# Expert tiles of a mixture of experts: rows turned three tiles ahead, second product two behind, and separate waits for the gate and up products

## The chip, the cores and the metric

The kernel runs on one core of a Trainium2 chip. The metric is the device time in microseconds of one execution. Engines: TensorE (PE, with its weight loads PEld), VectorE (DVE), ScalarE (ACT), GpSimd (POOL) and SyncE (SP), which here issues most of the DMAs.

## The reference

A graph attention layer and then a mixture of experts, with residuals. x is 128 x 128 x 128 in float32: 16,384 tokens of 128 values.

```
x = x + gnn(layernorm(x), adj, a0..a3)
# mixture of experts on h = layernorm(x):
probs   = softmax(h @ gate_w + gate_b)           # 16 experts
top_probs, top_idx = top_k(probs, 2)             # normalized to sum 1
hidden  = silu(h @ w1[e]) * (h @ w2[e])          # 128 -> 256
x = x + sum over the token's two experts of  weight * (hidden @ w3[e])
```

## The kernel before

Two parts follow one another. The first, until about 320 us, does the attention for 32 groups of 512 tokens and chooses the two experts of each token. GpSimd writes each finished row (x, its layer norm factors, its gates, its places) to its place in `first_list` in HBM by an indirect DMA (L574), so that rows of one expert lie together.

The second part, which the change touches, has two rounds: in round 0 each token's first expert, in round 1 its second. A round has 72 tiles of 256 rows (`TILES`): 48 "whole" ones with rows of one expert, 8 "lone" and 16 "mixed" ones with two halves of different experts. The first 36 tiles of a round are all whole; the other kinds are spread over the second half. Rows live in 12 slots `xin` (`S`). For a tile j, in slot u:

- SP loads its rows (L434, L438) when the slot is free (`s_z[u]`), and copies the expert's w1 and w2 from `wts` to `we` (L428).
- In round 0, VectorE applies the layer norm (L982), two tiles ahead of its own position; round 1 finds normed rows in `second_list`.
- TensorE turns the rows (two transposes, L1152), one tile ahead, into `psX`; ScalarE copies them to `xT` (L684).
- TensorE makes gate and up products (L1138) into `psG` and `psU`; ScalarE applies silu (L680); VectorE multiplies to `hid` (L977).
- TensorE makes the second product (L1162) into `psY`, one tile behind; VectorE adds gate times `psY` to the rows in `xin` (L990), called y below.
- GpSimd writes the rows out with two indirect DMAs, to `second_list` (L586) in round 0 and to the output (L598) in round 1, and their landing frees the slot.

Each engine runs the tiles in order through its own instruction queue; `done(eng, sems, n, u, d)` waits until the thing counted by `sems` is done for the tile d places away. In TensorE's queue the order for tile j is: gate and up products of j, turn of j+1, second product of j-1. `psX`, `psG`, `psU` and `psY` have two buffers each, `xT`, `silu` and `hid` too. Round 1's loads begin only after the rows of round 0 have been written. In tiles 3 to 35 of round 0, ScalarE also issues padding DMAs.

Of the kernel before, what the change touches and what calls it, by code (L numbers as in the profile page):

```python
# [5 lines left out]
def gnn_then_moe(nc: bass.Bass, x, adj, a0, a1, a2, a3, gate_w, gate_b, w1, w2, w3, out):  # L6
# [12 lines left out]
    P = 128  # L19
    B, N, D = x.shape  # L20
# [11 lines left out]
    HC = H // P  # L32
# [46 lines left out]
    with ctx:  # L79
# [126 lines left out]
        xT = sb("xT", [P, 2, W2])  # L206
        silu = sb("silu", [P, 2, HC * W2])
        hid = sb("hid", [P, 2, HC * W2])
# [132 lines left out]
        def tiles(eng, body, ahead, r, turns=1, between=None):  # L341
# [4 lines left out]
            def fixed(j):  # L346
                body(j // S, j % S, lambda d: first <= j + d < end)
            at, last = first // S + turns, (end - 2) // S
            for j in range(first - ahead, at * S):
                fixed(j)  # L350
                if between:
                    between(j)
            with eng.Fori(at, last) as n:
                for u in range(S):
                    body(n, u, lambda d: True)
            for j in range(last * S, end + 1):
                fixed(j)
# [144 lines left out]
        def _(pool):  # L502
# [77 lines left out]
            def first_out(n, u, on):  # L580
# [11 lines left out]
            def second_out(n, u, on):  # L592
# [11 lines left out]
            tiles(pool, first_out, 0, 0)  # L604
            tiles(pool, second_out, 0, 1)
# [5 lines left out]
        def _(act):  # L611
# [63 lines left out]
            def tile(n, u, on):  # L675
                w = u % 2
                if on(0):
                    done(act, s_hid, n, u, -2)
                    done(act, s_G, n, u, 0)
                    nc.scalar.activation(silu[:, w, :], psG[w], ACT.Silu).then_inc(s_silu[u % TURNS], 1)  # L680
                if on(1):
                    done(act, s_U, n, u, -1)
                    done(act, s_xTp, n, u, 1)
                    nc.scalar.activation(xT[:, 1 - w, :], psX[1 - w][:, 0:W2], ACT.Copy  # L684
                                         ).then_inc(s_xT[(u + 1) % TURNS], 1)
# [21 lines left out]
            tiles(act, tile, 1, 0, 3, table_and_pads)  # L707
            tiles(act, tile, 1, 1)
# [3 lines left out]
        def _(dve):  # L712
# [258 lines left out]
            def tile(r, n, u, on):  # L971
                w = u % 2
                if on(0):
                    done(dve, s_Y, n, u, -2)
                    done(dve, s_U, n, u, 0)
                    done(dve, s_silu, n, u, 0)
                    v.tensor_tensor(hid[:, w, :], silu[:, w, :], psU[w], ALU.mult).then_inc(s_hid[u % TURNS], 1)  # L977
                if on(2) and r == 0:
                    k = (u + 2) % S
                    wait_in(dve, n, u, 2)  # L980
                    for t in range(2):
                        last = v.tensor_scalar(xin[:, k, t, ROW:ROW2], xin[:, k, t, 0:D], xin[:, k, t, RSTD:RSTD + 1],  # L982
# [230 lines left out]
```

## Time and profile before

| | us |
|---|---|
| three timed runs, median | 904.5 (900.31 to 905.47) |
| span of the profiled execution | 903.2 |
| first part, until the first expert product | 0 to 324 |
| round 0, round 1 | 324 to 609, 613 to 888 |
| PE, POOL, DVE, ACT busy | 728.9, 516.0, 505.2, 421.3 |

The profile gives no time of its own for what lies around the span of its execution; the span is 1.3 us below the median of the timed runs. A row of a group has the line, engine, operation and tiles, the count, then busy time and mean of one, then the idle time before it and what ended it.

### The profile page before, as it was taken

How to read it: one execution, taken by the hardware profiler on the slowest of the kernel's cores; microseconds unless marked ns; L12 is line 12 of the kernel's file. 1: busy time of each engine (PE TensorE's matmuls, PEld its weight loads, DVE VectorE, ACT ScalarE, POOL GpSimd, SP SyncE). 2: the span in 40 equal slices, each digit the busy share in tenths (PEclk: the TensorE clock that was granted, in tenths of full speed). 3: DMA queues.
4: the chain of work that ended last, by engine and by line, in shares of the span. 5: the costliest groups of instructions: out<-in, count | busy, mean ns of one | idle time of the engine just before them, and what ended most of it. 6: DMA issues, size and time to landing. Idle time of an engine off the chain costs nothing.

```text
span 903.2 us, 17720 instructions
## 1 busy us (share of the span) xinstructions
PE 728.9 (81%) x4422; PEld 588.4 (65%) x4423; DVE 505.2 (56%) x1706; ACT 421.3 (47%) x1011; POOL 516.0 (57%) x670
## 2 busy tenths in 40 slices
PE   4899989998999638777787887788788887788872
PEld 2465656565655527667776887787777777788772
DVE  3789999999999834444453444343333323333331
ACT  7999999999998212222222222222222222222220
POOL 3337877777777674555554554455455444445553
PEclk9999999999999759999999899999999989999997
DMA  5234444423230045767765555527765546555620
GB/s 152 77 99 130 136 135 132 117 80 101 78 90 32 25 129 182 214 203 226 230 226 173 166 167 192 178 84 233 243 195 182 159 161 191 170 161 175 198 75 1
DMA packets 127460, 133.26 MB, mean 148 GB/s; under 512 B 16362, under 2 KB 98545, under 8 KB 127378
## 3 DMA queue, kind: packets, MB, share of 16 engines
q1 hardware_dynamic: 107008, 94.66, 34.7%
q0 software_dynamic: 15616, 34.38, 11.1%
q10 hardware_dynamic: 4754, 3.25, 1.2%
q8 instruction: 36, 0.59, 0.3%
q14 instruction: 46, 0.38, 0.1%
HBM read 52.28 MB, written 41.19 MB: 103 GB/s over the span
## 4 chain that ended last, share of the span: by engine, by line
PE 51%; ACT 25%; issue 18%; another core or an unknown queue 3%; DVE 1%; POOL 1%; DMA 0%; ACTq 0%; POOLq 0%; DVEq 0%
PE psS L1138 30%; PE bank L1162 14%; ACT late L636 8%; ACT h L668 5%; ACT late L644 5%; ACT late L626 4%; PE bank L1152 4%; ACT late L652 1%; PE bank L1038 1%; PE bank L1085 1%; ACT hT L634 1%; PE bank L1054 1%; ACT x1T L662 1%; POOL out_dram L598 1%
## 5 line engine op out<-in xcount | busy, mean ns | idle before, releaser
L1138 PE MATMUL psS<-xT,late 128*128 128x256 f32 (+1 forms) x1280 | 261.2, 353 | 97.5 <-issue 95.6
L1138 PEld LDWEIGHTS psS<-xT,late 128*128 128x128 f32 x1280 | 205.5, 197 | 124.5 <-issue 107.3
L680 ACT ACTIVATE silu<-psS 128x512 f32<-128x512 f32 x144 | 86.0, 597 | 308.7 <-remote 142.2
L586 POOL DMA_INDIRECT second_list<-xin x144 | 142.1, 987 | 135.4 <-DVE xin L990 101.2
L598 POOL DMA_INDIRECT out_dram<-xin x144 | 141.5, 983 | 132.7 <-DVE xin L990 92.4
L977 DVE TENSOR_TENSOR hid<-silu,psS 128x512 f32<-128x512 f32 x144 | 99.1, 688 | 206.2 <-PE psS L1138 80.6
L990 DVE SCALAR_TENSOR_TENSOR xin<-bank,xin 128x128 f32<-128x128 f32 x288 | 87.4, 345 | 137.7 <-remote 112.7
L1162 PE MATMUL bank<-wts,hid 128*128 (+1 forms) x1152 | 159.1, 283 | 1.0 <-DVE hid L977 0.6
L574 POOL DMA_INDIRECT first_list<-stage,slot x128 | 127.4, 995 | 49.4 <-issue 38.2
L1162 PEld LDWEIGHTS bank<-wts,hid 128*128 128x128 f32 x1152 | 147.5, 200 | 1.3 <-issue 1.3
L1025 PE MATMUL psS<-late,hT 128*128 128x512 f32 x256 | 117.9, 603 | 2.8 <-ACT late L636 2.8
L684 ACT ACTIVATE xT<-bank 128x256 f32<-128x256 f32 x144 | 55.0, 382 | 119.1 <-PE bank L1152 43.1
L789 DVE TENSOR_REDUCE late<-psS 128x512 f32<-128x2048 f32 x32 | 72.9, 2279 | 12.6 <-PE psS L1030 11.9
L1025 PEld LDWEIGHTS psS<-late,hT 128*128 128x128 f32 x256 | 46.9, 194 | 49.3 <-issue 46.3
L636 ACT ACTIVATE late<-bank,acol 128x512 f32<-128x512 f32 x128 | 77.2, 693 | 0.0
L1152 PE MATMUL bank<-ident,xin 128*128 128x128 f32 x288 | 58.3, 286 | 1.0 <-issue 1.0
L557 POOL TENSOR_TENSOR norm<-veps,minus_half 128x8 f32<-128x8 f32 (+1 forms) x37 | 55.8, 1507 | 0.0
L668 ACT ACTIVATE h<-X,norm 128x128 f32<-128x128 f32 x128 | 52.5, 489 | 1.3 <-POOL norm L561 1.3
L644 ACT ACTIVATE late<-late,negmax 128x128 f32<-128x128 f32 x128 | 50.0, 415 | 5.8 <-DVE negmax L820 5.8
L1152 PEld LDWEIGHTS bank<-ident,xin 128*128 128x128 f32 x288 | 41.6, 150 | 12.3 <-issue 2.6
L1138 PE MATMUL psS<-xT,wts 128*128 128x128 f32 x256 | 35.7, 298 | 13.6 <-ACT xT L684 11.0
L982 DVE TENSOR_SCALAR xin<-xin 128x128 f32<-128x128 f32 x144 | 44.9, 358 | 0.0
(156 smaller groups left out, 829.3 us busy)
## 6 DMA issues: line engine op xcount, KB each, us to landing
late<-wts SPq DMA_DIRECT2D x160, 256.0 KB
xin<-second_list SPq DMA_DIRECT2D x48, 262.0 KB
X<-in_x_dram SPq DMA_DIRECT2D x32, 256.0 KB
late<-in_adj_dram SPq DMA_DIRECT2D x32, 256.0 KB
xin<-first_list SPq DMA_DIRECT2D x48, 134.0 KB
xin<-second_list SPq DMA_DIRECT2D x48, 131.0 KB
wts<-in_L_ffn_w_dram SPq DMA_DIRECT2D x48, 128.0 KB
xin<-first_list SPq DMA_DIRECT2D x48, 67.0 KB
```

Source lines behind the costliest of these rows:

```text
L574: pool.indirect_dma_start(first_list[:, :], bass.IndirectOffsetOnAxis(ap=slot[:, g % SB, t:t + 1], axis=0), stage_v(g % SB)[:, t, :], None ...
L586: pool.indirect_dma_start(second_list[:, :], bass.IndirectOffsetOnAxis(ap=xin[:, u, k, SLOT1:SLOT1 + 1].bitcast(i32), axis=0), xin[:, u, k ...
L598: pool.indirect_dma_start(out_rows[:, :], bass.IndirectOffsetOnAxis(ap=xin[:, u, k, DEST:DEST + 1].bitcast(i32), axis=0), xin[:, u, k, 0:D ...
L636: last = nc.scalar.activation(hTa[s % 2][:, k, :], psT[:, :], ACT.Copy, scale=acol[:, k:k + 1])
L644: last = nc.scalar.activation(prob[:, p, c], prob[:, p, c], ACT.Exp, bias=negmax[:, p, t:t + 1], accum_out=rowsum[:, p, t:t + 1])
L668: last = nc.scalar.activation(h[:, g % HB, t * D:(t + 1) * D], X[:, g % XQ, t * D:(t + 1) * D], ACT.Identity, scale=norm[:, b, 0, t, 0:1], ...
L977: v.tensor_tensor(hid[:, w, :], silu[:, w, :], psU[w], ALU.mult).then_inc(s_hid[u % TURNS], 1)
L990: last = v.scalar_tensor_tensor(at, psY[1 - w][:, t * D:(t + 1) * D], xin[:, k, t, GATE[r]:GATE[r] + 1], at, ALU.mult, ALU.add)
L1025: mm(psS[:, t, :], hT[:, g % 2, t * D:(t + 1) * D], hTa[g % 2][:, :, t * D:(t + 1) * D], start=True, stop=False)
L1138: last = mm(out[:, c * W2 + rows.start:c * W2 + rows.stop], at[:, half * H + c * P:half * H + (c + 1) * P], xT[:, w, rows], start=True, st ...
L1152: last = nc.tensor.transpose(psX[1 - w][:, t * P:(t + 1) * P], xin[:, k, t, ROW:ROW2], ident[:, :])
L1162: last = mm(psY[1 - w][:, t * D:(t + 1) * D], hid[:, 1 - w, at:at + P], wts[:, ds(e[t] * EW + (UP + c * D), D)], start=(c == 0), stop=(c = ...
```

## The change

TensorE turns rows three tiles ahead (`LEAD`) and makes the second product two behind (`LAG`). ScalarE's copy to `xT` and VectorE's norm move with it (norm four ahead), and y two tiles behind. `xT` has three buffers and `hid` four, both placed in `X`, which the first part no longer needs. The gate product waits for silu of two tiles back, the up product for hid of two tiles back; before, both waited for hid. At the start of a round tiles 0 and 1 are turned first, then 2, then 3 and 4.

```diff
+        HIDS, XTS = 4, 3
-        hid = sb("hid", [P, 2, HC * W2])
+        hid = X[:, 0:HIDS, :]
+        xT = X[:, HIDS:XQ, :].rearrange("p a (b w) -> p (a b) w", w=W2)
+        LEAD, LAG = 3, 2
+        def turned_after(i):
+            return {-1: [0, 1], 0: [2], 1: [LEAD, LEAD + 1]}.get(i, [i + LEAD])
+        def normed_after(i):
+            return {-1: [0, 1, 2], 0: [LEAD, LEAD + 1]}.get(i, [i + LEAD + 1])
+        def offsets(i, after):
+            if i is None:
+                return [after(S)[0] - S]
+            return [k - i for k in after(i) if k < TILES]
...
# ScalarE
-                if on(1):
-                    done(act, s_U, n, u, -1)
-                    done(act, s_xTp, n, u, 1)
+                for d in offsets(i, turned_after):
+                    k = (u + d) % S
+                    done(act, s_U, n, u, d - XTS)
+                    done(act, s_xTp, n, u, d)
...
# VectorE
-                    done(dve, s_Y, n, u, -2)
+                    done(dve, s_Y, n, u, -HIDS)
...
-                if on(-1):
-                    k = (u - 1) % S
-                    done(dve, s_Y, n, u, -1)
+                if on(-LAG):
+                    k = (u - LAG) % S
+                    done(dve, s_Y, n, u, -LAG)
...
# TensorE
-                    done(pe, s_hid, n, u, -2)
                     done(pe, s_xT, n, u, 0)
                     parts = weights()
-                    for half, out, s_out in ((0, psG[w], s_G), (1, psU[w], s_U)):
+                    for half, out, s_out, s_free in ((0, psG[u % 2], s_G, s_silu), (1, psU[u % 2], s_U, s_hid)):
+                        done(pe, s_free, n, u, -2)
...
-                    if weights:
-                        done(pe, s_xT, n, u, -1)
+                for d in offsets(i, turned_after):
+                    k = (u + d) % S
+                    done(pe, s_xT, n, u, d - 2)
...
-                    done(pe, s_y, n, u, -3)
-                    done(pe, s_hid, n, u, -1)
+                    k = (u - LAG) % S
+                    done(pe, s_y, n, u, -LAG - 2)
+                    done(pe, s_hid, n, u, -LAG)
```

## Rows read from the trace of the kernel before

**Rows 1.** The page: busy time, share of the span and instructions.
```profile
PE 728.9 (81%) x4422; PEld 588.4 (65%) x4423; DVE 505.2 (56%) x1706; ACT 421.3 (47%) x1011; POOL 516.0 (57%) x670
```

**Rows 2.** Windows, four expert stretches: start:end, length, busy (count), clock, DMA share, GB/s.
```profile
344.70:468.30 123.60, 100.61 (x613) 89.29 (x613) 63.20 (x189) 31.70 (x68) 65.12 (x66) 1.00 0.70 220
468.30:606.10 137.80, 112.56 (x816) 106.23 (x815) 61.50 (x175) 33.80 (x70) 69.06 (x70) 0.94 0.49 162
612.90:748.00 135.10, 112.29 (x641) 99.47 (x641) 44.67 (x106) 34.53 (x72) 68.78 (x70) 0.94 0.62 194
748.00:886.00 138.00, 112.14 (x837) 106.12 (x838) 46.08 (x109) 34.36 (x71) 71.59 (x73) 0.96 0.49 155
```

**Rows 3.** Groups of instructions, 330 us to the end.
```profile
L1138 PE MATMUL psS<-xT,late 128*128 128x256 f32 (+1 forms) x1272 | 257.4, 351 | 96.3 <-issue 94.4 <-ACT xT L684 1.8
L977 DVE TENSOR_TENSOR hid<-silu,psS 128x512 f32<-128x512 f32 x144 | 99.1, 688 | 206.2 <-PE psS L1138 80.6 <-remote 68.6 <-ACT silu L680 41.4
L990 DVE SCALAR_TENSOR_TENSOR xin<-bank,xin 128x128 f32<-128x128 f32 x288 | 87.4, 345 | 137.7 <-remote 112.7 <-PE bank L1162 21.2 <-issue 3.5
...
L1138 PE MATMUL psS<-xT,wts 128*128 128x128 f32 x256 | 35.7, 298 | 13.6 <-ACT xT L684 11.0 <-issue 2.6
```

**Rows 4.** Timeline of PE, round 0: start, length, what [idle before <-releaser].
```profile
421.54 1.97 PE L1138 MATMUL psS<-xT,late 128*128 128x256 f32 x8 [1.57 <-issue]
...
424.45 1.89 PE L1138 MATMUL psS<-xT,late 128*128 128x256 f32 x8
...
426.40 1.06 PE L1162 MATMUL bank<-wts,hid 128*128 x8
428.91 1.97 PE L1138 MATMUL psS<-xT,late 128*128 128x256 f32 x8 [1.45 <-issue]
```

**Rows 5.** Timeline of ACT, the same stretch.
```profile
422.74 0.60 ACT L680 ACTIVATE silu<-psS 128x512 f32<-128x512 f32 x1 [1.30 <-issue]
...
427.94 0.60 ACT L680 ACTIVATE silu<-psS 128x512 f32<-128x512 f32 x1 [3.74 <-remote]
428.43 0.38 ACT L684 ACTIVATE xT<-bank 128x256 f32<-128x256 f32 x1
```

**Rows 6.** Timeline of POOL, the same stretch, the first, last and next issue of a run.
```profile
421.93 0.98 POOL L586 DMA_INDIRECT second_list<-xin  x1 [2.64 <-DVE xin L990]
...
425.80 0.98 POOL L586 DMA_INDIRECT second_list<-xin  x1 [0.30 <-issue]
429.29 0.98 POOL L586 DMA_INDIRECT second_list<-xin  x1 [2.50 <-DVE xin L990]
```

**Rows 7.** Timeline, round 1, a long stall; POOL's first and sixth issue.
```profile
628.60 0.98 POOL L598 DMA_INDIRECT out_dram<-xin  x1 [2.61 <-DVE xin L990]
...
631.12 1.89 PE L1138 MATMUL psS<-xT,late 128*128 128x256 f32 x8
...
635.11 0.98 POOL L598 DMA_INDIRECT out_dram<-xin  x1 [0.30 <-issue]
...
636.85 0.60 ACT L680 ACTIVATE silu<-psS 128x512 f32<-128x512 f32 x1 [5.97 <-remote]
...
638.16 2.64 PE L1138 MATMUL psS<-xT,late 128*128 128x256 f32 x8 [4.03 <-issue]
```

**Rows 8.** Timeline of SP's queue, round 0, row loads of three tiles.
```profile
387.06 0.01 SPq L438 DMA_DIRECT2D xin<-first_list  x1
...
391.04 0.38 SPq L438 DMA_DIRECT2D xin<-first_list  x1
...
393.01 0.38 SPq L438 DMA_DIRECT2D xin<-first_list  x1
```

**Rows 9.** Line L438, round 0, 345.4 to 443.3 us; the next load is at 443.40.
```profile
L438 SPq DMA_DIRECT2D xin<-first_list x30: 5/384/722, 345.5 to 438.3; - x30
```

**Rows 10.** Line L438, round 1, 613 to 660.5 us; the next load is at 660.62.
```profile
L438 SPq DMA_DIRECT2D xin<-second_list x18: 3/385/707, 613.3 to 658.4; - x18
```

**Rows 11.** SP's waits, 717 to 850 us: total, times, longest.
```profile
SPq L414 <- DMA out_dram<-xin: 16.1, 9, 3.6
```

More of the change, by code:

```diff
@@ L339, in norms, with tiles @@
             return slice(0 if s + 1 < G else 1, 2 if 0 <= s - 4 < G else 1)
-        def tiles(eng, body, ahead, r, turns=1, between=None):
+        LEAD, LAG = 3, 2
[7 more added lines that the diff above has]
+            return [k - i for k in after(i) if k < TILES]
+        def tiles(eng, body, r, behind, turns=1, between=None):
             first, end = r * TILES, (r + 1) * TILES
             def fixed(j):
-                body(j // S, j % S, lambda d: first <= j + d < end)
+                body(j // S, j % S, j - first, lambda d: first <= j + d < end)
             at, last = first // S + turns, (end - 2) // S
-            for j in range(first - ahead, at * S):
+            for j in range(first - 1, at * S):
                 fixed(j)
@@ L354, in tiles @@
                 for u in range(S):
-                    body(n, u, lambda d: True)
-            for j in range(last * S, end + 1):
+                    body(n, u, None, lambda d: True)
+            for j in range(last * S, end + behind):
                 fixed(j)
@@ L705, in table_and_pads @@
                     pad(1, second_list, ROW2, j - 4 - E)
-            tiles(act, tile, 1, 0, 3, table_and_pads)
-            tiles(act, tile, 1, 1)
+            tiles(act, tile, 0, 0, 3, table_and_pads)
+            tiles(act, tile, 1, 0)
         @block.vector
@@ L995, in _, with lists_after @@
-            tiles(dve, lambda n, u, on: tile(1, n, u, on), 2, 1)
+            def lists_after(j):
+                for i in (-2, -1) if j < 0 else (j,):
+                    lists(i)
+            tiles(dve, lambda n, u, i, on: tile(0, n, u, i, on), 0, LAG, 1, lists_after)
+            tiles(dve, lambda n, u, i, on: tile(1, n, u, i, on), 1, LAG)
         @block.tensor
@@ L1161, in tile @@
                             at = c * W2 + t * P
-                            last = mm(psY[1 - w][:, t * D:(t + 1) * D], hid[:, 1 - w, at:at + P],
+                            last = mm(psY[k % 2][:, t * D:(t + 1) * D], hid[:, k % HIDS, at:at + P],
                                       wts[:, ds(e[t] * EW + (UP + c * D), D)],
```

65 lines of the change are left out of this document (29 added, 36 removed).

## The prediction

> **What bounds the kernel now.** I read the page first, then the windows, then the groups, then the order of time inside one stall. TensorE is busy 81% of the span, GpSimd 57% [rows 1]. The change touches only the expert part, so the windows matter more: the four expert stretches take 123.6, 137.8, 135.1 and 138.0 us, 534.5 together, and TensorE is busy 437.6 of them, at a granted clock of 1.00, 0.94, 0.94 and 0.96 [rows 2]. They hold 34, 35, 36 and 36 tiles (a tile of one expert has 18 matmul records, and 613 / 18 is 34), so a tile costs 3.64, 3.94, 3.75 and 3.83 us.
>
> The groups say where TensorE is idle: before L1138, the gate product, 96.3 + 13.6 = 109.9 us, and practically nowhere else [rows 3]. "Issue" hides the reason; the order of time shows it [rows 4]. Tile A starts at 421.54, tile B at 424.45: 2.91 us with no gap. The next starts at 428.91, after 1.45 us idle. What it waited for is its turned rows: ScalarE copies them (L684) at 428.43, right after a silu at 427.94 [rows 5]. That silu is the odd one. In tile A it ran 1.20 us after the product began (422.74 against 421.54), in tile B 3.49 us after (427.94 against 424.45), "remote" being all the profile names. So the notice that the product was done came about 2.3 us late, and the copy queued behind the silu, and tile C behind the copy, paid for it.
>
> Why late? Just then GpSimd had issued four indirect DMAs without a pause, 421.93 to 425.80 [rows 6]. In the second round it is the same with six of them (628.60 to 635.11): silu 5.97 us idle, TensorE 4.03 us idle, and the tile after it slower, 2.64 us against 1.89 for eight products, because the clock had been lowered after the pause [rows 4, 7]. The reading: while GpSimd issues more than about two in a row, TensorE's notices are held until the run is nearly over. This is inferred from a coincidence that repeats, not shown.
>
> SP is held too. Its row loads stand at 387.06, 391.04 and 393.01: one tile's issue took 3.98 us in such a stretch, the next 1.97 [rows 8]. Over 30 loads of the first round it goes 345.5 to 443.4, 3.26 us a tile [rows 9]; at the start of the second round 18 loads take 47.3 us, 2.63 each [rows 10]. In the last stretch it waits 16.1 us of 133 for slots [rows 11], so it works about (133 - 16.1) / (133 / 3.83) = 3.37 us a tile there, where tiles of two experts need up to four transfers. SP is thus the second engine close to the pace.
>
> **The change, step by step.** Counts of instructions stay: 288 turns, the same products, activations and DMAs. New are one more wait a tile on TensorE (gate waits for silu of two tiles back, up product for hid of two tiles back, each its own) and other addresses for hid and xT (in X). Where nothing waits, tiles follow at 2.91 us [rows 4], so waits already met show no price; I take 0, with 0.05 us x 144 = 7 us as my upper bound. For the addresses no row gives a reason either way: 0.
>
> *Rows turned three ahead.* Tile C's gate product no longer waits for a copy made in tile B. Its own condition is now silu(i) before gate(i+2). The gate product ends about 0.95 us after its start (half of 1.89), so from there to gate(i+2) are 2 x 2.91 - 0.95 = 4.87 us; less the silu's 0.60, 4.3 us of lateness can pass unseen [rows 4, 5]. The up product likewise: 5.82 + 0.95 - 1.89 - 0.69 for hid = 4.2 us [rows 3, 4]. Queued behind its new wait stand this tile's up product, the turn of tile i+3 and the second product, and behind those everything of the next tile; but the hid it asks for was asked for before, ahead of the gate product, so the wait is only moved back by half a product. Lateness was 2.3 us in the run of four, and 636.85 - 631.12 - 1.20 = 4.5 us in the run of six [rows 7]. So nearly all of the 1.45 us and most of the 4.03 us go.
>
> *Second product two behind.* It then waits for hid of two tiles back, and y(i-4) must have freed its bank; both are 2.91 us older than before. The y, GpSimd's DMA and the slot's reuse come one tile later. That costs one more product group at the end (1.06 us [rows 4]) and, between the rounds, where the second round's loads wait for the last written rows, one tile, about 3 us. Sum +4. In return the tiles ahead of stretch 1, which have the same waits, should end about 3 us sooner (two pauses like the 1.45 of [rows 4]). +1 is left.
>
> If that were all, TensorE would run 141 tiles at 2.91: 410 us for 534.5, a gain of 124. It is not all, for two others come next.
>
> *GpSimd next.* Four issues from 421.93 hold things until 427.94, 6.0 us, so 1.50 us each in effect, though a record says 0.98 [rows 5, 6]; six give (636.85 - 628.60) / 6 = 1.38 [rows 7]. A tile needs two: 2.8 to 3.0 us, floor. Today a pair of tiles takes 7.37 us (421.54 to 428.91): 6.0 and then 1.35 until the next issue at 429.29 [rows 4 to 6]. With TensorE ahead, the following tile's result is there when the run ends, and the pause shrinks to about 0.7 us, the two operations of one y at 345 ns each [rows 3]. Bursts of two tiles: 6.7 / 2 = 3.35; of three: 9.7 / 3 = 3.23. I take 3.3.
>
> *SP next.* Denser runs slow SP. In round one it does 3.26 us a tile with the present density [rows 9], and now needs each load two tiles sooner, so it leaves no reserve to eat: stretch 1 can't go below about 3.3. In the stretches of lone and mixed tiles it worked 3.37 a tile; with holds half of the time instead of a third I take 3.7 and 3.65 (free 1.97 and held 3.98 [rows 8] average 2.98 for a whole tile, 13% above the 2.63 of [rows 10]; 3.37 scaled by this gives 3.8, and I take a little less since a third of these tiles are whole).
>
> Sum, in us: stretch 1, 34 x 3.3 = 112.2, -11.4. Stretch 2, 35 x 3.7 = 129.5, -8.3. Stretch 3, 36 x 3.35 = 120.6, -14.5. Stretch 4, 36 x 3.65 = 131.4, -6.6. Together -40.8, +1 from the lag: about -40. Clock dips are inside the tile times of before and are not counted again. The profiled execution has a span of 903.2, only 1.3 under the median of 904.5, so 904.5 - 40 = 864.5; I say 864.
>
> **A page against this row.** SP is held beside GpSimd [rows 8]. The Trainium skill, "DMA: Bandwidth & Descriptors", section "SWDGE vs HWDGE vs iDMA", says that GpSimd writes its descriptors into rings in SBUF and that DMAs issued from SP never touch that path. By that rule SP would have no price here; the 3.98 against 1.97 us speaks against reading it so.
>
> **Rivals.**
> (a) *The hold grows with the run.* If notices stay held as long as GpSimd finds work, more work ready at once means longer holds, and TensorE waits just as long, only later: 7.37 us per two tiles is then a property of the holds. For it: six in a row held longer than four. Against: the pause of 1.35 us after each run is due to TensorE's stop. Time 897 to 906. Chance 0.09.
> (b) *SP starves: slower.* If GpSimd's runs never end, SP falls to its held pace of 3.98 us, and the transpose of tile i+3, standing in TensorE's queue ahead of second products, blocks all. Over stretches 1 and 3 that is 34 x (3.98 - 3.64) + 36 x (3.98 - 3.75) = +20 us, with 2 and 4 as before: 904 + 20 = 924. It decides once SP's pace is above 3.8, the mean tile of before. Against: starved tiles give GpSimd less to issue, which frees SP. Chance 0.06.
> (c) *SP costs nothing extra.* Its reserve of loaded slots carries it, and GpSimd alone sets 3.3 a tile throughout: 141 x 3.3 = 465, -69, 836; at GpSimd's floor of 3.0: 423, -111, of which the start and the turn of the rounds take some 10: 804. This is also where the page's rule would lead. For it: today SP gains 3.64 - 3.26 = 0.38 us a tile on TensorE, 11 us over 30 tiles [rows 2, 9], more in the second round [rows 10], and late in the round it has so far got ahead that it waits for slots [rows 11]. Chance 0.25, most of it at 825 to 845.
> (d) My forecast, both next engines bind in part: 0.60, own range 848 to 882.
>
> Beyond about 0.5% (4.5 us) a measurement of this kernel tells a difference from none: its three runs lie 5 us apart. Faster: (c), (d), and a third of (a), 0.88. Same: most of (a), 0.06. Slower: (b), 0.06. Range 822 to 894: it reaches into (c) and to the edge of (a), and leaves out both ends, 0.2 together.
>
> **What the profile after would show.** Right: the idle before L1138 falls from 110 to under 50 us; silus still show "remote" waits of 2 to 6 us, now without a TensorE gap behind them; GpSimd's pauses for y shrink; SP shows no slot waits. TensorE's busy sum stays. Wrong, if the remote waits vanish (then they were not GpSimd's), if TensorE's idle only moves to the turns (L1152), waiting for loads, beyond 50 us (SP, b), or if pairs still take 7.4 us (a). The clock's dips should go from the middle on, since pauses of 4 us vanish.

## The result and the profile after

The changed kernel takes 888.9 us (median of four runs, 881.8 to 894.4) against 902.4 for the kernel before beside it (900.0 to 905.5). The ratio is 0.986, 95% interval 0.981 to 0.991. It is faster, by 13.5 us, where 40 were forecast. The profiled execution is the slowest of the four (894.4), with a span of 892.6 us against 903.2. On the page only TensorE's busy time rose, by 12.5 us; the others moved by 5.4 us or less [rows 1]:

```profile
PE 741.4 (83%) x4422; PEld 588.5 (66%) x4423; DVE 501.3 (56%) x1706; ACT 415.9 (47%) x1011; POOL 519.7 (58%) x670
```

The windows over the same tiles as before (start:end, length, then busy time and count of PE, PEld, DVE, ACT and POOL, then clock, DMA share and GB/s):

```profile
342.30:467.20 124.90, 111.15 (x614) 94.63 (x614) 63.15 (x187) 33.50 (x71) 63.00 (x64) 0.91 0.69 213
467.20:600.70 133.50, 114.02 (x812) 105.04 (x811) 58.38 (x167) 31.07 (x67) 69.86 (x71) 0.94 0.53 171
615.90:736.40 120.50, 107.73 (x637) 93.56 (x636) 40.94 (x99) 32.05 (x72) 61.60 (x63) 0.98 0.66 204
736.40:866.00 129.60, 110.70 (x812) 102.14 (x811) 43.23 (x108) 31.89 (x70) 69.22 (x72) 0.97 0.58 179
```

Between the first gate products of the same tiles, before and after:

| stretch | before | after | change | forecast |
|---|---|---|---|---|
| until tile 2 of round 0 | 344.7 | 342.3 | -2.4 | -3 |
| stretch 1 (tiles 2 to 36) | 123.6 | 124.9 | +1.4 | -11.4 |
| stretch 2 (36 to 71) | 137.9 | 133.6 | -4.3 | -8.3 |
| turn of the rounds (71 to 0) | 6.7 | 15.2 | +8.5 | +4, with the end |
| stretch 3 (0 to 36) | 135.1 | 120.4 | -14.7 | -14.5 |
| stretch 4 (36 to 71) | 135.5 | 129.7 | -5.8 | -6.6 |
| end (from 71) | 19.8 | 26.6 | +6.8 | (in the +4) |
| span | 903.2 | 892.6 | -10.6 | -40 |

(Differences are taken before rounding; stretch 4 ends here where tile 71 starts, a little sooner than in [rows 2].)

Round 1 came out as forecast. The missing 29 us are in stretches 1 and 2, 12.8 and 4.0, and at the two places where a round ends, 12 together with the start.

The groups from 330 us to the end, to be held against [rows 3] (`hid` and `xT` now bear the name X):

```profile
L1158 PE MATMUL psS<-X,late 128*128 128x256 f32 (+1 forms) x1270 | 260.8, 354 | 5.4 <-issue 4.3 <-DMA xin<-second_list 1.1
...
L1181 PE MATMUL bank<-wts,X 128*128 (+1 forms) x1152 | 166.3, 286 | 29.4 <-issue 15.6 <-DVE xin L1007 11.9 <-ACT silu L696 1.1
...
L992 DVE TENSOR_TENSOR X<-silu,psS 128x512 f32<-128x512 f32 x144 | 98.5, 684 | 238.4 <-remote 139.0 <-ACT silu L696 42.8 <-PE psS L1158 39.8
...
L696 ACT ACTIVATE silu<-psS 128x512 f32<-128x512 f32 x144 | 86.1, 598 | 267.4 <-remote 172.2 <-PE psS L1158 61.8 <-issue 33.2
L1171 PE MATMUL bank<-ident,xin 128*128 128x128 f32 x282 | 58.6, 288 | 51.5 <-issue 38.4 <-DMA xin<-second_list 7.0 <-DVE xin L999 3.1
```

The idle time before the gate and up products is gone, 109.9 us down to 6.4. But 51.5 us now stand before the turn (L1171) and 29.4 before the second product (L1181). Of the 51.5, 29.6 lie in stretches 1 and 2 and 5.0 in stretches 3 and 4; the rest is at the starts of the rounds. The "remote" waits of silu and hid have not gone: 172.2 and 139.0 us.

**Round 1: a long hold no longer stops TensorE.** Timeline, one run of six issues:

```profile
658.18 0.98 POOL L615 DMA_INDIRECT out_dram<-xin  x1 [2.84 <-DVE xin L1007]
...
658.64 1.89 PE L1158 MATMUL psS<-X,late 128*128 128x256 f32 x8
...
661.48 1.89 PE L1158 MATMUL psS<-X,late 128*128 128x256 f32 x8
...
664.33 1.58 PE L1158 MATMUL psS<-X,late 128*128 128x256 f32 x6
664.62 0.98 POOL L615 DMA_INDIRECT out_dram<-xin  x1 [0.30 <-issue]
...
667.06 0.61 DVE L1007 SCALAR_TENSOR_TENSOR xin<-bank,xin 128x128 f32<-128x128 f32 x2 [3.63 <-remote]
...
667.18 0.60 ACT L696 ACTIVATE silu<-psS 128x512 f32<-128x512 f32 x1 [2.65 <-remote]
...
668.55 0.98 POOL L615 DMA_INDIRECT out_dram<-xin  x1 [2.95 <-DVE xin L1007]
...
669.16 1.89 PE L1158 MATMUL psS<-X,late 128*128 128x256 f32 x8
```

Six issues start at 658.18 to 664.62. Meanwhile TensorE makes three tiles (658.64, 661.48, 664.33) while the y and the silu of the last come only at 667.06 and 667.18; the last two products of the third come late, by 0.33 us each, and its turn and second product follow late too: the next tile starts 4.83 us after the third (669.16), where undisturbed ones follow at 2.84. So the run costs TensorE 2.0 us. In [rows 7] a run of six cost 4.03 us of idle time and a slower tile behind it. GpSimd starts again at 668.55, so three tiles take 10.37 us, 3.46 each.

**Round 0: the turn waits for the norm.** Timeline of stretch 1:

```profile
418.73 1.89 PE L1158 MATMUL psS<-X,late 128*128 128x256 f32 x8
...
420.09 0.98 POOL L603 DMA_INDIRECT second_list<-xin  x1 [0.30 <-issue]
...
422.44 0.69 DVE L992 TENSOR_TENSOR X<-silu,psS 128x512 f32<-128x512 f32 x1 [5.73 <-remote]
...
423.04 0.60 DVE L999 TENSOR_SCALAR xin<-xin 128x128 f32<-128x128 f32 x2
...
423.74 0.66 PE L1171 MATMUL bank<-ident,xin 128*128 128x128 f32 x2 [3.12 <-issue]
...
426.03 3.62 PE L1158 MATMUL psS<-X,late 128*128 128x256 f32 x8
```

The hid product of the tile at 415.89 waits 5.73 us for a held notice (422.44). The norm (L999) stands behind it in VectorE's queue and runs right after it, at 423.04. The turn of the rows three tiles ahead waits for this norm, and TensorE stands for 3.12 us. Its next eight gate and up products take 3.62 us where 1.89 is usual: the clock had fallen. It is the norm throughout round 0: all 15 pauses of over 0.5 us before the turn in stretches 1 and 2, 27.9 us together, end 0.10 us after a norm ended, so none of them waits for a load of rows.

In stretch 1 the granted clock is 0.91, before it was 1.00 [rows 2]. Not all of this comes from such pauses. The clock had fallen at the start of the round already, and here it stays at half for the first 9 us of stretch 1 (a window, as above):

```profile
342.30:351.30 9.00, 7.76 (x24) 6.07 (x24) 4.06 (x15) 2.02 (x5) 0.23 (x1) 0.50 0.47 142
```

In the trace before it was back at full speed when stretch 1 began. The other dips of this stretch come with its three longest pauses, 3.32, 3.12 and 1.94 us, which end at 397.6, 423.7 and 449.1 us: over 395 to 405, 420 to 430 and 447 to 457 us the granted clock is 0.83, 0.66 and 0.83.

**Where a round ends** a hold lies between the last products and the last writes. Timeline of the turn of the rounds, then of the end:

```profile
598.41 0.98 POOL L603 DMA_INDIRECT second_list<-xin  x1 [0.30 <-issue]
...
600.59 0.69 DVE L992 TENSOR_TENSOR X<-silu,psS 128x512 f32<-128x512 f32 x1 [5.68 <-remote]
601.19 0.60 DVE L1007 SCALAR_TENSOR_TENSOR xin<-bank,xin 128x128 f32<-128x128 f32 x2
...
602.67 0.98 POOL L603 DMA_INDIRECT second_list<-xin  x1 [3.28 <-DVE xin L1007]
...
609.73 0.01 SPq L455 DMA_DIRECT2D xin<-second_list  x1
...
612.02 0.66 PE L1171 MATMUL bank<-ident,xin 128*128 128x128 f32 x2 [4.47 <-DMA xin<-second_list]
```

```profile
871.04 0.98 POOL L615 DMA_INDIRECT out_dram<-xin  x1 [0.30 <-issue]
871.81 0.69 DVE L992 TENSOR_TENSOR X<-silu,psS 128x512 f32<-128x512 f32 x1 [4.96 <-remote]
873.23 1.13 DVE L1007 SCALAR_TENSOR_TENSOR xin<-bank,xin 128x128 f32<-128x128 f32 x4 [0.74 <-remote]
...
874.23 2.07 PE L1181 MATMUL bank<-wts,X 128*128 x8 [4.21 <-DVE xin L1007]
...
881.15 0.98 POOL L615 DMA_INDIRECT out_dram<-xin  x1 [0.30 <-issue]
```

VectorE gets to y at 601.19 and 873.23 only, after it has waited 5.68 and 4.96 us for a held hid. All writes of the last tiles follow, and what waits for them.

### The profile page after: what moved, and what is told of

It reads as the page before. It is cut to its first block, busy times and chain, and to the rows that moved or that the text cites. A ratio compares the mean times of both kernels' runs of the same rounds, so it can differ in the third digit from the quotient of the medians.

```text
span 892.6 us, 17721 instructions
## 1 busy us (share of the span) xinstructions
PE 741.4 (83%) x4422; PEld 588.5 (66%) x4423; DVE 501.3 (56%) x1706; ACT 415.9 (47%) x1011; POOL 519.7 (58%) x670
## 4 chain that ended last, share of the span: by engine, by line
PE 37%; ACT 23%; issue 16%; another core or an unknown queue 8%; SPq 7%; DVE 3%; DMA 2%; POOL 1%; ACTq 0%; DVEq 0%; POOLq 0%
PE psS L1158 18%; PE bank L1181 10%; ACT late L653 7%; ACT h L685 5%; ACT late L661 5%; ACT late L643 3%; PE bank L1171 3%; SPq L445 2%; SPq L451 2%; PE psS L1046 2%; PE bank L1059 1%; SPq L455 1%; PE bank L1075 1%; DVE X L992 1%
## 5 line engine op out<-in xcount | busy, mean ns | idle before, releaser
L1158 PE MATMUL psS<-X,late 128*128 128x256 f32 (+1 forms) x1280 | 265.4, 356 | 6.1 <-issue 5.0
L992 DVE TENSOR_TENSOR X<-silu,psS 128x512 f32<-128x512 f32 x144 | 98.5, 684 | 238.4 <-remote 139.0
L1158 PEld LDWEIGHTS psS<-X,late 128*128 128x128 f32 x1280 | 213.0, 203 | 28.0 <-issue 9.2
L615 POOL DMA_INDIRECT out_dram<-xin x144 | 141.5, 983 | 125.4 <-DVE xin L1007 88.3
L696 ACT ACTIVATE silu<-psS 128x512 f32<-128x512 f32 x144 | 86.1, 598 | 267.4 <-remote 172.2
L1181 PE MATMUL bank<-wts,X 128*128 (+1 forms) x1152 | 166.3, 286 | 29.4 <-issue 15.6
L1181 PEld LDWEIGHTS bank<-wts,X 128*128 128x128 f32 x1152 | 147.5, 198 | 40.0 <-issue 39.5
L701 ACT ACTIVATE X<-bank 128x256 f32<-128x256 f32 x144 | 55.2, 384 | 147.8 <-remote 79.9
L1171 PE MATMUL bank<-ident,xin 128*128 128x128 f32 x288 | 60.5, 291 | 52.4 <-issue 39.3
L1171 PEld LDWEIGHTS bank<-ident,xin 128*128 128x128 f32 x288 | 39.1, 150 | 72.1 <-issue 64.5
L805 DVE TENSOR_REDUCE late<-psS 128x512 f32<-128x2048 f32 x32 | 72.9, 2279 | 12.5 <-PE psS L1051 11.6
L999 DVE TENSOR_SCALAR xin<-xin 128x128 f32<-128x128 f32 x144 | 45.1, 367 | 1.3 <-DMA xin<-first_list 0.8
L1075 PE MATMUL bank<-h,probT 128*128 128x128 f32 x256 | 38.0, 293 | 8.6 <-ACT probT L674 4.4
## 6 DMA issues: line engine op xcount, KB each, us to landing
xin<-second_list SPq DMA_DIRECT2D x48, 131.0 KB
```

Of the source, the lines that this page charges most:

```text
L615: pool.indirect_dma_start(out_rows[:, :], bass.IndirectOffsetOnAxis(ap=xin[:, u, k, DEST:DEST + 1].bitcast(i32), axis=0), xin[:, u, k, 0:D ...
L992: v.tensor_tensor(hid[:, u % HIDS, :], silu[:, u % 2, :], psU[u % 2], ALU.mult).then_inc(s_hid[u % TURNS], 1)
L1158: last = mm(out[:, c * W2 + rows.start:c * W2 + rows.stop], at[:, half * H + c * P:half * H + (c + 1) * P], xT[:, u % XTS, rows], start=Tr ...
L1171: last = nc.tensor.transpose(psX[k % 2][:, t * P:(t + 1) * P], xin[:, k, t, ROW:ROW2], ident[:, :])
L1181: last = mm(psY[k % 2][:, t * D:(t + 1) * D], hid[:, k % HIDS, at:at + P], wts[:, ds(e[t] * EW + (UP + c * D), D)], start=(c == 0), stop=( ...
```

## The experiments

**One chip of five is different.** The experiments were run in five sets, each on a chip of its own, with the kernel before beside it. It took 760.5 us in one of them and 901.8 to 915.0 in the others, which is where it stood in the result too (902.4). Ratios are to the kernel before of the same set. The sets are called A (760.5 us), B (911.3), C (906.8), D (915.0) and E (901.8). The first part takes 323 to 325 us in every trace; the difference is in the expert part. Since each chip was seen in one set only, that it is the chip and not the time is inferred. A notice is called late, or held, when a semaphore event of an instruction comes over 0.3 us after the instruction's end in the trace.

### Set A: where no notice is late

Norm first, for `e1` (from tile 4 on the norm stands before the hid product):

```diff
+                norm_first = i is None or i >= 4
+                if r == 0 and norm_first:
+                    norm()
                 if on(0):
...
-                if r == 0:
+                if r == 0 and not norm_first:
                     norm()
```

`e2` has `LEAD, LAG = 3, 1`, `e3` has `LEAD, LAG = 1, 2`, `e4` has `for k in range(1)` in the writes of round 1, with the waits on their landing adapted.

> The changed kernel, with one thing moved: from tile 4 of round 0 on, VectorE applies the layer norm of tile i+4 before hid of tile i, not after it. Theory N (in round 0 the turn of tile i+3 stands in TensorE's queue behind a norm that VectorE makes only after hid of tile i-1, so a late notice of the up product still stops TensorE, and stretch 1 gained nothing): the idle before L1171-type turns in round 0 goes, stretch 1 (tiles 2 to 36) falls from 125 to about 114 us, stretch 2 by 3 to 5 us, the whole to 872 to 878. Rival S (stretch 1 is set by SyncE's pace of loads): the turns wait for loads instead, stretch 1 stays at 120 to 125 us, the whole at 886 to 890.

> The changed kernel with the second product one tile behind again (LAG 1), rows still turned three ahead. Theory L (the lag of two costs at the turn of the rounds and at the end, and gives nothing in between, since what stopped TensorE was the turned rows): the way from the last gate product of round 0 to the first of round 1 falls from 15.2 to about 10 us, the end from 26.6 to about 22 us, the stretches stay, the whole is 878 to 882. Rival (the lag is what lets TensorE run on while notices are late, since the second product waits for hid): stretches 3 and 4 rise by 10 us or more together, the whole is 895 or above.

> The changed kernel with rows turned only one tile ahead (LEAD 1, norm two ahead), the second product still two behind and the waits of gate and up products still their own. Theory (the turn three ahead carries the gain of round 1): round 1's stretches go back to about 135 and 135 us and the idle is before the gate product again; with the losses of the lag at the ends of the rounds the whole is 900 to 915. Rival (the waits of their own and the lag carry it): stretches 3 and 4 stay near 120 and 130, the whole 885 to 892.

> The changed kernel; in round 1 GpSimd issues only the first of the two indirect DMAs of each tile (the other half of the output rows isn't written), in round 0 both. Theory G (runs of GpSimd's issues hold TensorE's notices and SyncE): with runs half as long the remote waits of silu in round 1 nearly vanish, tiles follow at 2.9 to 3.0 us in stretch 3 (105 us for 120) and stretch 4 (108 for 130), the end falls from 26.6 to about 17 us. Rival (the late notices have another source, such as DMA traffic or SyncE's issues, which stay): stretch 3 and 4 move by less than 5 us each.

Measured, against 760.5: norm first 766.9 (ratio 1.009, 1.006 to 1.011), lag one 762.8 (1.003, 1.001 to 1.005), turn one ahead 763.3 (1.0045, 1.003 to 1.006), half writes 755.6 (single run). The changed kernel itself was not run in this set. None of the gains and losses that the expectations name appears, and the traces show why: there is no stall to remove. Windows of turn one ahead, the second halves of its two rounds, then its groups of the expert part:

```profile
427.10:527.90 100.80, 100.80 (x817) 97.74 (x816) 60.15 (x175) 34.36 (x70) 70.42 (x70) 1.00 0.71 227
638.00:738.80 100.80, 100.80 (x817) 97.74 (x816) 45.45 (x105) 34.36 (x70) 69.59 (x71) 1.00 0.71 220
```

```profile
L603 POOL DMA_INDIRECT second_list<-xin x144 | 143.6, 997 | 54.6 <-issue 51.0 <-DVE xin L1007 3.6
...
L992 DVE TENSOR_TENSOR X<-silu,psS 128x512 f32<-128x512 f32 x143 | 98.5, 688 | 168.0 <-PE psS L1158 160.6 <-ACT silu L696 7.4
...
L615 POOL DMA_INDIRECT out_dram<-xin x144 | 141.5, 983 | 69.4 <-issue 61.3 <-DVE xin L1007 8.0
...
L696 ACT ACTIVATE silu<-psS 128x512 f32<-128x512 f32 x142 | 84.8, 597 | 198.6 <-PE psS L1158 194.1 <-issue 4.5
```

TensorE is busy all of the 100.8 us, at full clock; a tile takes 2.88 us. No "remote" wait is left. And GpSimd hardly pauses, 0.38 us before an issue on average (54.6 us for 144): in this trace up to 62 indirect issues follow one another at most 1.36 us apart. So a run of issues by itself does not make a notice late. With nothing to hide, the later end of lag two is a plain cost: the end takes 22.3 us with lag two (norm first and turn one alike), 19.7 with lag one.

### Set B: the result again, and half the writes

> The changed kernel as it is, to see it beside the kernel before on the chip of these experiments. If the kernel before takes about 760 us there, as in the first four experiments, with no remote waits, both kernels have TensorE busy without a gap at 2.84 us a tile, and the change costs what the lag costs at the turn of the rounds and at the end: 1.000 to 1.008 of before. If it takes about 900 us, with remote waits: 0.98 to 0.99. Rival: the gain is there too without the late notices, from the turns' own order: 0.99 or less at 760 us.

> The kernel before as it is, for its trace on this chip. Theory (the 1.45 us gaps of the trace shown are made by late notices alone): where silus run 1.2 to 1.4 us after their product begins, no gap before gate products, 2.84 to 2.91 us a tile, the four stretches about 101 us each. Rival (the loop of turn, copy and gate product stops TensorE by itself): gaps before gate products of 0.3 us or more a tile remain, 10 us a stretch.

> The kernel before; in round 1 GpSimd issues only the first of the two indirect DMAs of each tile (the other half of the output rows isn't written). If notices are late here (before at 900 us), theory G expects stretches 3 and 4 at 105 to 110 us for 135, 138 and the remote waits gone; rival: no change. If before is at 760 us: the same stretches as before, only the end 2 to 5 us sooner.

The changed kernel repeats its ratio, 0.986 (0.982 to 0.991). The kernel before, traced here once more (909.5 us, single run), has late notices, so what would be left without them is read in its version with fewer writes. With half the indirect writes in round 1 it takes 836.1 us (single run), against 911.3. Its round 1, groups from 620 to 820 us:

```profile
L1138 PE MATMUL psS<-xT,late 128*128 128x256 f32 (+1 forms) x600 | 118.3, 344 | 4.0 <-issue 4.0
...
L977 DVE TENSOR_TENSOR hid<-silu,psS 128x512 f32<-128x512 f32 x69 | 47.5, 688 | 88.7 <-PE psS L1138 56.0 <-ACT silu L680 24.8 <-remote 5.5
...
L680 ACT ACTIVATE silu<-psS 128x512 f32<-128x512 f32 x69 | 41.2, 597 | 97.5 <-PE psS L1138 97.5
```

The "remote" waits of silu are gone, 5.5 us are left before hid, and 4.0 us of idle time before the product. Stretches 3 and 4 take 107.6 and 100.8 us, where the kernel before of this set has 135.8 and 137.1. Round 0, with all its writes, stays at 126.5 and 137.8.

### Set C: each part of the change where notices are late

The four kernels of set A again.

> The norm of the tile ahead stands before the hid product on VectorE from tile 4 on (round 0 alone has norms). Theory, to be tested where the notices from TensorE are late (before about 905 us): in round 0 the turn of tile i+3 waits for a norm that stands behind the late hid of tile i-1. Then the stretch from tile 2 to 36, 124.9 us after the change, falls to about 114, the next, 133.6, to about 125, round 1 stays at about 120 and 130, and the whole comes to about 875 (ratio 0.96 to 0.975). Rival: GpSimd's runs of issues pace the tiles there (TensorE's queue is held whatever stands ahead of it); then the stretches stay within 3 us of 124.9 and 133.6 and the ratio at 0.985. If this call's chip shows no late notices (before about 760 us), the ratio is about 1.005 as it was.

> Rows turned three tiles ahead, the second product one tile behind as before. If the gain comes from the turn taken ahead, the stretches of round 1 stay near 120 and 130 us, the turn of the rounds falls from 15.2 to about 10 and the end from 26.6 to about 22: ratio about 0.975. If it comes from the second product being two tiles behind (it can wait for a late hid without holding the gate products), the stretches go back to near 135 and the ratio to about 1. Where before is about 760 us, about 1.003.

> The second product two tiles behind, rows turned one tile ahead as before. By the theory on record (the stall before the gate products waits for the copy of the turned rows, whose notice is late) the stretches of round 1 go back to about 135 us each, with the later end kept: ratio 1.00 to 1.015. By the rival that GpSimd's own issue rate sets the pace, lead and lag are both worth little: stretches within 4 us of 120 and 130, ratio 0.985. Where before is about 760 us, about 1.0045.

> The changed kernel, with one of the two indirect writes of each tile in round 1 left out (its rows aren't written, so part of the output is not computed). The theory of GpSimd's issue runs says that round 1's stretches fall from 120 and 130 us to about 101 to 104 each, as they did in the kernel before (to 107.6 and 100.8), so a whole of about 840; that the changed one gains nothing over the kernel before once the notices are on time. If the changed kernel's stretches stay above 115, something other than the issues holds it.

| kernel | ratio (95%) | str. 1 | str. 2 | turn | str. 3 | str. 4 | end |
|---|---|---|---|---|---|---|---|
| changed (profile of the result) | 0.986 | 124.9 | 133.6 | 15.2 | 120.4 | 129.7 | 26.6 |
| changed (set B) | 0.986 (0.982 to 0.991) | 130.0 | 133.3 | 12.0 | 121.4 | 130.2 | 25.0 |
| norm first | 0.976 (0.969 to 0.983) | 120.4 | 124.2 | 10.5 | 123.7 | 132.1 | 25.1 |
| lag one | 0.983 (0.976 to 0.989) | 128.3 | 131.9 | 10.9 | 123.7 | 125.8 | 23.8 |
| turn one ahead | 1.0045 (1.000 to 1.009) | 127.2 | 136.2 | 9.5 | 135.0 | 132.6 | 24.0 |
| half writes | 0.919 (0.914 to 0.925) | 125.4 | 128.1 | 13.5 | 103.3 | 100.3 | 11.7 |

*The lead is the whole gain.* With the turn back at one ahead the ratio is 1.0045, and the idle time is back before the products (groups, 330 us on):

```profile
L1158 PE MATMUL psS<-X,late 128*128 128x256 f32 (+1 forms) x1272 | 269.1, 362 | 86.2 <-ACT X L701 50.0 <-issue 36.2
...
L1171 PE MATMUL bank<-ident,xin 128*128 128x128 f32 x284 | 58.7, 291 | 0.9 <-DMA xin<-second_list 0.9
L1158 PE MATMUL psS<-X,wts 128*128 128x128 f32 x256 | 34.1, 290 | 12.0 <-ACT X L701 7.8 <-issue 4.3
```

86.2 + 12.0 = 98.2 us, and the releaser named is the copy of the turned rows, as read in the kernel before. *The lag adds nothing that can be told here:* without it 0.983 (0.975 was expected), with it 0.986, intervals overlapping. In round 0 the pauses of about 3 us stand before the turn in both.

*Norm first* gives round 0 (stretches 1 and 2) 244.6 us, where lag one of the same set has 260.2 and the changed kernel 258.5 and 263.3. Its two windows:

```profile
341.30:461.70 120.40, 108.11 (x614) 89.05 (x613) 62.29 (x185) 32.33 (x71) 63.68 (x65) 0.97 0.71 215
461.70:585.90 124.20, 111.81 (x812) 103.98 (x811) 59.15 (x171) 30.86 (x67) 68.83 (x70) 0.95 0.59 188
```

The clock in stretch 1 is 0.97, not 0.91. The pauses of over 2.5 us, two in stretch 1 of the changed kernel, four and three in its repetitions in sets B and D, don't occur. The expectation of 114 us is missed, though: stretch 1 still takes 120.4, and TensorE's idle time in it is 12.3 us, against 13.8 in the profile of the result and 17 to 18 in the two repetitions. The changed kernel itself was not run in this set.

*Half the writes* bring the changed kernel to 103.3 and 100.3 us in round 1; the kernel before with half the writes has 107.6 and 100.8, so the change gains little there (4.3 and 0.5 us in single profiles) once the notices are on time.

### Set D: both mends together, and what in the writes it is

`g1` joins norm first and lag one; `g0` is the changed kernel. `g2` in round 1:

```diff
-                        pool.indirect_dma_start(
-                            out_rows[:, :],
-                            bass.IndirectOffsetOnAxis(ap=xin[:, u, k, DEST:DEST + 1].bitcast(i32), axis=0),
-                            xin[:, u, k, 0:D], None, bounds_check=TOKENS - 1, oob_is_err=False
+                        pool.dma_start(first_list[ds(at + k * P, P), 0:D],
+                                       xin[:, u, k, 0:D]).then_inc(s_z[u], 16)
```

(`at` goes on by 256 rows a tile.) `g3` leaves out `copy_weights` in round 1, and TensorE's waits for them.

> Norm ahead of the hid product from tile 4 on, rows turned three tiles ahead, second product one tile behind. If the two costs found so far add up (norm first took 17 us off round 0, lag one some 4 us off the turn of the rounds and the end), the ratio is about 0.970 (about 878 where before is 905). If lag one gives its gain back in round 0, where the product then waits for the late hid, the ratio is that of norm first alone, 0.976. Where before is about 760 us: 1.005.

> The changed kernel, to be compared within this call: 0.986 where before is about 905. Where before is about 760 us and no notice is late, the stalls that it takes away aren't there, and the later end and turn of the rounds remain: 1.00 to 1.01.

> The changed kernel; in round 1 GpSimd writes each tile's rows with two plain DMAs of the same bytes to places in the first list instead of two indirect ones to the output (the output is then not written). If the late notices come from the indirect issues (GpSimd works out the addresses of 128 rows), they go from round 1, and its stretches fall from 120 and 130 us to about 101 to 104. If any DMA that GpSimd issues does it, or the write traffic itself, they stay at 120 and 130.

> The changed kernel; in round 1 the copies of the gate and up weights on SP's queue are left out (the tiles multiply by the weights that round 0 left). If GpSimd's indirect issues alone make the notices late, round 1's stretches stay within 5 us of 120 and 130. If the late notices come from the sum of DMA traffic or of SP's issues with GpSimd's, they fall towards 101 us.

Both changes: ratio 0.974 (0.969 to 0.979); the changed kernel beside it 0.9835 (0.978 to 0.989). In the two profiles round 0 takes 255.5 and 262.2 us, the turn of the rounds 10.9 and 13.7, the end 19.8 and 25.0; round 1 gives 3.9 us back. Round 0 gains less than norm first alone did, and the trace shows why: its pauses of over 2.5 us, three in stretch 1 and two in stretch 2, now stand before the second product (L1186), which waits for the held hid of the tile just before. So, by the traces, lag two and norm first belong together; either alone leaves TensorE one instruction that a hold stops. The whole times don't show it: 0.976 with both, 0.974 and (in set E) 0.9805 with norm first and lag one, intervals overlapping. Plain writes: 841.7 us (single run) against 915.0, stretches 3 and 4 105.4 and 100.3 us. Its groups of round 1:

```profile
L694 ACT ACTIVATE silu<-psS 128x512 f32<-128x512 f32 x71 | 42.4, 598 | 98.0 <-PE psS L1156 96.6 <-issue 1.3
...
L616 POOL DMA_DIRECT2D first_list<-xin x136 | 73.4, 541 | 128.8 <-DVE xin L1005 123.7 <-issue 2.2
```

The bytes are the same and the writes are still GpSimd's, but not one notice of TensorE is late in this round. A plain issue takes 0.54 us, an indirect one 0.98, so this does not part the form from the time that it takes. Without the weights copies: 881.2 us (single run), stretches 3 and 4 115.9 and 121.5 us, and the late notices stay (silu waits 73.4 us for "remote"). So the copies are not what holds the notices, but they cost 6.5 and 10.5 us of the two stretches against the changed kernel's profile of this set (122.4 and 132.0). That is more than the 5 us that the expectation allowed.

### Set E: runs of issues broken up

On top of norm first and lag one (`h0`), GpSimd waits in both rounds before the writes of tile j for the up product of j+2:

```diff
                     done(pool, s_y, n, u, -1)
+                    if on(1):
+                        done(pool, s_U, n, u, 1)
```

In `h2` it waits for the gate product of j+2 before the first write, for the up product before the second.

> Control of this call: norm first, rows turned three tiles ahead, second product one behind. 0.974 as before where before is about 905; 1.005 where it is about 760.

> As the control; GpSimd waits before the two writes of tile j for the notice of the up product of j+2, so a run can't go on past a tile while a notice is held. If a hold lasts as long as the unbroken run, holds are cut to some 3 us, which three tiles of lead and the buffers of silu and hid hide: stretches of round 1 from about 124 and 133 to 105 to 115 us, ratio 0.94 to 0.955. If a hold depends on the number of indirect writes and not on their run, the stretches stay, or grow by the later writes: ratio 0.97 to 0.985.

> As the control; GpSimd waits before the first write of tile j for the notice of the gate product of j+2 and before the second for that of the up product, so that never two issues follow one another while a notice is held. If the length of the run makes the holds, no hold is above 1.5 us and tiles take about 3.3 us or less: ratio 0.93 to 0.95. If each issue holds notices for its own 1.4 us whatever stands between, GpSimd and TensorE wait for one another in turns and a tile takes about 3.8 us or more: ratio 0.98 to 1.02.

Measured, against 901.8: control 883.7 (0.9805, 0.974 to 0.987), by tile 860.9 (0.954, 0.948 to 0.961), by issue 863.6 (0.957, 0.950 to 0.963). By tile, stretches 1 to 4 take 118.0, 124.4, 120.3 and 121.6 us, against the control's 124.0, 127.9, 123.2 and 131.0. Timeline of its POOL:

```profile
642.09 0.98 POOL L619 DMA_INDIRECT out_dram<-xin  x1 [1.75 <-PE psS L1167]
...
645.96 0.98 POOL L619 DMA_INDIRECT out_dram<-xin  x1 [0.30 <-issue]
649.45 0.98 POOL L619 DMA_INDIRECT out_dram<-xin  x1 [2.50 <-DVE xin L1016]
...
653.31 0.98 POOL L619 DMA_INDIRECT out_dram<-xin  x1 [0.30 <-issue]
656.02 0.98 POOL L619 DMA_INDIRECT out_dram<-xin  x1 [1.72 <-issue]
```

Runs now have mostly four issues: those of six fall from 19 to 5 in the expert part, and the holds of over 4 us there from 29 to 13 (a hold is a stretch in which TensorE's instructions end and their semaphore events come over 0.3 us later). The number of holds does not fall, 70 and 84 in the expert part. The ratio lies in the range expected, the stretches of round 1 above their 105 to 115 us: shorter runs make shorter holds, not fewer. By issue misses its expectation: 0.957 for 0.93 to 0.95, and 24 of its holds still last over 4 us where none over 1.5 was expected, for most issues still come in runs of three to five. These two are the fastest versions that compute everything; neither was run where no notice is late.

## Why the prediction was wrong

The measured 888.9 us lie inside the stated range of 822 to 894, near its slow edge, but outside the 848 to 882 of the forecast's own case (d), and the gain is a third of the forecast.

**What binds, and the stall that goes: right.** The stall before L1138 was put down to the copy of the turned rows, queued behind a late silu. It fell from 109.9 to 6.4 us, and turn one ahead brought it back to 98.2 and the ratio to 1.0045. But the prediction also named as a sign of being wrong that the idle time moves to the turns, beyond 50 us, waiting for loads. It did move there, 51.5 us, and in round 0 it waits for the norm, not for loads.

**"This is inferred, not shown": half right.** GpSimd's indirect writes are needed for the late notices: half of them, or plain ones instead, and they are gone (half writes on the changed kernel, plain writes) or nearly so (half writes on the kernel before). That is shown for round 1, where they were taken away; the plain ones are also shorter, so form and time are not parted. They are not enough: set A had up to 62 in a row and no late notice. What differs between the chips stays open.

**Slack of 4.3 us: right, but the lateness was taken as fixed.** Rival (a) said that a hold grows with the run. It does. In round 1 runs averaged 3.1 issues before and 5.4 after (22 of 27 runs have six). There are fewer holds, 34 before and 27 after, but they last 102 us together before and 150 after: 3.0 and 5.6 us each. With three tiles of lead they cost TensorE little, so the time that (a) gave, 897 or more, was still wrong.

**GpSimd next, 3.3 us a tile: right sum, one term wrong.** Stretches 3 and 4 were forecast at -14.5 and -6.6 and came at -14.7 and -5.8. In the prediction's terms the run of six shown above held things from 658.18 to 667.18, 9.0 us, which is the forecast 1.50 an issue (the issues themselves follow every 1.29 us, and the held notice comes 1.5 us after the last one ends). But the pause after it was to shrink to 0.7 us and is 1.37 (667.18 to 668.55), as long as the 1.35 of before, since y was held too and has yet to be made. So three tiles take 10.37 us, not 9.7, and the 21 tiles from 658.6 to 730.7 us take 3.43 us each. That stretch 3 still comes to the forecast 3.35 is luck in part: its other 15 tiles, at its two ends, take 3.22.

**The step that failed: stretch 1, "34 x 3.3 = 112.2, -11.4"** (and 4 of stretch 2's 8.3). The prediction asked what the gate product and the second product wait for after the change, and not what the turn waits for. In round 0 that is a norm that stands behind the hid product of a held tile, so a hold goes through VectorE to TensorE past all of the lead. Round 1 has no norms, and there the forecast held. Two things added up in stretch 1. TensorE's idle time fell from 23.0 to 13.8 us only (length less busy time), nearly all before the turn. And its busy time rose from 100.6 to 111.2 for the same products, at a clock of 0.91 instead of 1.00: fewer pauses, but longer ones (16 before, none over 1.7 us; 11 after, up to 3.3).

The second is the larger. With the busy time that the prediction held fixed ("TensorE's busy sum stays"), 112.2 us left room for 11.6 us of idle time; so of the 12.7 us too many, 10.5 are busy time and 2.2 idle. The clock was the term put at nothing: its dips were held to be "inside the tile times of before", and in stretch 1 before there were none. Of these 10.5 us about 4.5 (an estimate: 9.0 us at half the clock) are the low clock of the round's start, which reached into the stretch in this profile; in the two repetitions it did so for 2.8 and 2.9 us only. The rest goes with the long pauses.

That the long pauses are the norm's doing is shown by their place, 0.10 us after a norm's end, and by norm first, where they are gone. The size is loose: norm first takes 15.6 us off round 0 against lag one in set C, and together with lag one 6.7 against the changed kernel in set D; single profiles of round 0 differ by some 5 us from one another. In stretch 1 of norm first it came to 120.4 us, not 112.2. Nearly all of these 8 us are again busy time, 108.1 us at a clock of 0.97; for about half of it the trace shows a low clock, why the products took longer for the rest stays unexplained.

**The lag, "+4 and -3": a mis-sized term.** Start, turn of the rounds and end together gave +12.9, not +1. One tile later was counted at TensorE's pace. But the last y is behind a held hid, and this wait, 5.0 to 5.7 us, isn't hidden where no further tile follows. The start gained the forecast amount. Lag one has 10.9 and 23.8 us at these places, the changed kernel 15.2 and 26.6, and 12.0 and 25.0. How much of this is lag and how much chance of where a hold falls, single profiles can't part; where none is late lag two costs 2.6 us at the end.

**SP next: it carried a price, of another size.** SP's slot waits, 16.1 us at L414 in [rows 11], are 0 at its counterpart for landed output writes and 2.5 at the next line, as foreseen. Without the weights copies 6.5 and 10.5 us of stretches 3 and 4 go. But the pace put down to SP, 3.65 and 3.7 us a tile, is no floor: norm first has stretch 2 at 124.2 us, below the forecast 129.5, and runs broken up by tile have stretch 4 at 121.6, below 131.4, with all of SP's transfers. That stretch 4 came near its forecast therefore does not show that SP set it. The forecast that the clock's dips go was nearly right for round 1 (0.94 and 0.96 before, 0.98 and 0.97 after) and wrong for stretch 1.

The prediction weighed a page of the Trainium skill ("DMA: Bandwidth & Descriptors", section "SWDGE vs HWDGE vs iDMA"): DMAs issued from SP don't touch the path of GpSimd's. Set A agrees, where SP fed a tile every 2.88 us beside unbroken runs; [rows 8] show SP's issues slow beside GpSimd's, on a chip with late notices; whether that is the path which the page means, no run here shows.

## What to carry to other kernels

When work is moved ahead to hide a late result, list for every instruction moved what it waits for in its new place, through the queues of the other engines too: one operation behind a late one brings much of the delay back. Ask also what the clock will do: in stretch 1 fewer but longer pauses saved 9 us of idle time and cost 10.5 us at a lower clock. Slack covers a delay only while more work follows, so price the last tiles of each phase with the full delay. And before hiding a delay, look for what makes it: halving GpSimd's indirect writes in one of the rounds (half of the output is then missing) took the changed kernel from 0.986 to 0.919, while all that was won by order alone is 1.4 to 2.6%; a wait that breaks up its runs gave another 2.6%.

## What the runs showed that was not expected

- The same kernel takes 760 us on one chip and 902 to 915 on the four others and in the result, with the same first part (323 to 325 us). The difference goes with late notices: none in any trace on the former; on the others, in the profiles of the kernel before and the changed one, 60 to 76 stretches of them in the expert part, 226 to 270 us in all. Some 25 to 31 more lie in the first part, which is no longer for them.
- It is TensorE's semaphore events that are late: in the kernel before of set B, of 788 of TensorE's instructions that raise a semaphore the trace has an event for 678, and 281 of these are late; of ScalarE's 351 none, of VectorE's 724 one. About 30% of ScalarE's and 20% of VectorE's events are missing there, though, while in set A nearly all are present. Every run has its span recorded, so whether the recording has a part in the delays, none can tell.
- Indirect writes of 128 rows follow one another every 1.29 us, their records being 0.98 long; two a tile are 2.58 us of the 2.88 that a tile takes in set A. A plain write of the same bytes is 0.54 us.
